# Reordering the recurrent stage of a one-core decoder kernel: paired 64-row products, swapped low-rank operands, norms on ScalarE

## What is computed

```python
xa = _ln(x, ln1_w, ln1_b)
sx = concat([state[:, 1:2] - xa[:, :1], xa[:, :-1] - xa[:, 1:]], axis=1)
xxx = tanh((xa + sx * maa_x) @ maa_w1).reshape(b, l, 5, DM)          # DM = 32
xm = xa + sx * (maa_stack + einsum('blfd,fde->blfe', xxx, maa_w2))   # 5 mixes: k, w, v, r, g
w = exp(-exp(time_decay + tanh(xw @ td_w1) @ td_w2))
r, k, v, g = xr @ Wr.T, xk @ Wk.T, xv @ Wv.T, silu(xg @ Wg.T)
s = a + w_t * s ; out = r_t . (u * a + s)                            # a = k_t v_t, a scan over time
x1 = x + groupnorm(out) * g @ Wo.T
xc = _ln(x1, ln2_w, ln2_b)                                           # then shifted and mixed with ffn_maa_k, ffn_maa_r
return x1 + sigmoid(xr2 @ Wfr.T) * (square(relu(xk2 @ Wfk.T)) @ Wfv.T)
```

## Time and profile before

| | |
|---|---|
| median of 3 runs | 3513.13 us (3513.01 to 3519.1) |
| profiled execution | 3515.94 us, of which the span from first to last instruction is 3514.2 us |
| TensorE matmul busy | 3222.5 us, 92% of the span |
| VectorE, ScalarE, GpSimd busy | 50%, 32%, 26% of the span |
| mean granted TensorE clock | 0.975 of full speed |
| the recurrent stage | from about 1571 to 2480 us of the span |

### The profile page before, as it was taken

The page is one execution under the profiler, slowest core; times in us unless marked ns, Lnnn a source line. Parts: engine busy times, 40 slices in busy tenths (PEclk is TensorE's granted clock), DMA queues, the critical chain, the costliest instruction groups (busy, mean ns, idle before and its releaser), DMA issues. The chain is left out here.

```text
span 3514.2 us, 52783 instructions
## 1 busy us (share of the span) xinstructions
PE 3222.5 (92%) x19344; PEld 2128.6 (61%) x19344; DVE 1748.5 (50%) x2503; ACT 1131.0 (32%) x4052; POOL 900.5 (26%) x614
## 2 busy tenths in 40 slices
PE   7999899989999888867899999997799999899999
PEld 5665556557666555546666666664455555466675
DVE  4555556510000378864788888888264454400000
ACT  2444234412111366642232332332133333311111
POOL 2333233300000022223555555565100000100000
PEclk9999999999999899988999999999899999999999
DMA  4110321110000141111011111110130110101010
GB/s 164 43 41 32 119 89 56 34 66 12 24 15 21 40 159 48 44 62 40 26 46 37 36 49 37 36 46 28 60 128 32 33 41 22 49 19 36 21 33 12
DMA packets 104308, 170.19 MB, mean 48 GB/s; under 512 B 16512, under 2 KB 54016, under 8 KB 100736
## 3 DMA queue, kind: packets, MB, share of 16 engines
q1 hardware_dynamic: 99296, 124.58, 11.1%
q10 hardware_dynamic: 4896, 44.04, 3.1%
HBM read 135.03 MB, written 33.55 MB: 48 GB/s over the span
## 5 line engine op out<-in xcount | busy, mean ns | idle before, releaser
L2396 POOL TENSOR_TENSOR rec_S<-rec_S,rec_r_t 128x1024 f32<-128x1024 f32 x128 | 309.8, 2421 | 315.1 <-DVE rec_S L2677 315.1
L2677 DVE TENSOR_TENSOR_SCAN rec_S<-rec_decay,rec_S 128x1024 f32<-128x1024 f32 x128 | 321.9, 2515 | 22.7 <-ACT rec_S L2466 19.4
L2076 PE MATMUL mlp_bank<-mlp_src_t,region_a 128*128 128x256 f32 x1024 | 224.8, 382 | 3.1 <-ACT mlp_src_t L1997 3.1
L2076 PE MATMUL pmlp_bank<-pmlp_src_t,region_a 128*128 128x256 f32 x1024 | 224.9, 382 | 1.9 <-ACT pmlp_src_t L1997 1.9
L2088 PE MATMUL mlp_bank<-region_a,mlp_h_t 128*128 128x512 f32 x512 | 221.1, 592 | 0.0
L2088 PE MATMUL pmlp_bank<-region_a,pmlp_h_t 128*128 128x512 f32 x512 | 221.1, 592 | 0.0
L2076 PEld LDWEIGHTS mlp_bank<-mlp_src_t,region_a 128*128 128x128 f32 x1024 | 196.5, 192 | 33.3 <-issue 6.8
L2076 PEld LDWEIGHTS pmlp_bank<-pmlp_src_t,region_a 128*128 128x128 f32 x1024 | 196.5, 192 | 32.0 <-issue 5.5
L1505 ACT ACTIVATE group_scores<-group_scores,group_negmax 128x128 f32<-128x128 f32 x512 | 197.6, 391 | 28.6 <-DVE group_negmax L1599 18.7
L2043 DVE TENSOR_TENSOR mlp_y<-mlp_bank,mlp_xres 128x512 f32<-128x512 f32 x16 | 11.1, 691 | 375.4 <-PE mlp_bank L2088 375.4
L2043 DVE TENSOR_TENSOR pmlp_y<-pmlp_bank,pmlp_xres 128x512 f32<-128x512 f32 x16 | 11.1, 691 | 364.6 <-PE pmlp_bank L2088 364.6
(11 more groups left out here) (363 smaller groups left out, 6496.4 us busy)
## 6 DMA issues: line engine op xcount, KB each, us to landing
rec_vb<-v_by_head SPq DMA_DIRECT2D x32, 512.0 KB, 4.2
region_a<-in_C_w ACTq DMA_DIRECT2D x2, 4096.0 KB, 20.5
region_a<-in_G_w ACTq DMA_DIRECT2D x2, 4096.0 KB, 19.5
self_xres<-in_x SPq DMA_DIRECT2D x16, 256.0 KB, 2.6
rows_A<-self_xres SPq DMA_DIRECT2D x16, 256.0 KB, 2.0
cross_ctx_t<-in_ctx_t SPq DMA_DIRECT2D x16, 256.0 KB, 3.3
cross_xres<-rows_A SPq DMA_DIRECT2D x16, 256.0 KB, 2.6
rows_B<-cross_xres SPq DMA_DIRECT2D x16, 256.0 KB, 2.0
```

Source lines behind the costliest of these rows:

```text
L2076: product = nc.tensor.matmul(ph.bank(item)[:, i * TT:(i + 1) * TT], W1[:, c, f:f + 128], src_t[:, c, :, :], start=c == 0, stop=c == C - 1)
L2396: nc.gpsimd.tensor_tensor(S[u % 4][:, :, :], S[u % 4][:, :, :], bcast(r_t[:, s.k, UNITS[u][0], :], [128, JH, T], 1), ALU.mult)\
L2677: nc.vector.tensor_tensor_scan(St[:, :, :].rearrange(flat), decay[m][:, :, :].rearrange(flat), St[:, :, :].rearrange(flat), 0.0, ALU.mult, ...
```

## The change

The low-rank product makes `xa_t` stationary and streams the 160 weight columns, so that its result has time on the partitions; one tanh writes it into `low_rows`, where each mix has 64 columns (32 values, a one, zeros); TensorE transposes these back in three products (`low_rank_t`, bank a, use lt) and ScalarE copies them into `low` (`low_rank_copy`). The mixes are placed so that 1 and 2, 3 and 4, and 0 and the decay product lie in different halves of the partitions; they are issued alternately in pairs. The two norms are applied by ScalarE as scale and bias; for that VectorE also negates the mean, and GpSimd multiplies it by the power. ScalarE copies `xa_t` back into bank b, from where `shift_front` takes one operand; that bank is now freed by the shift, and `low_rank` no longer waits for it. `gate` on ScalarE stands ahead of `bonus`, `make_gate` on VectorE ahead of `inputs(7)`. On TensorE the transposes of `ahead` stand before `ffn_keys`, the second half of r and of g directly behind the first, the first half of the output projection ahead of `sum_heads(2)`, and `ffn_gate` is split 2, 1, 1. The load of the first column (SyncE) waits for the same point of the former sequence, counted by three, now the copy back into the bank. Some lines of indentation are removed in the cut diff:

```diff
@@ -2167,12 +2167,12 @@
     MIX_AT = {f: at for at, f in enumerate(MIX_ORDER)}
-    MIX_TILE = {0: (0, 0), 1: (0, 64), 2: (1, 0), 3: (1, 64), 4: (2, 0)}
+    MIX_TILE = {1: (0, 0), 2: (0, 64), 0: (1, 0), 3: (1, 64), 4: (2, 0)}
...
     NEWTON = 10
-    SETUP = 11
+    SETUP = 7
@@ -2227,7 +2228,7 @@
         banks = StepBanks("rec", sem, {b: ps(f"bank_{b}", [128, BANK]) for b in "abcdn"}, [
-("a", "mx", 0), ("b", "mix1", 0), ("a", "mix2", 0), ("n", "mean", 2),
+("a", "mx", 0), ("a", "lt", 0), ("b", "mix1", 0), ("a", "mix2", 0), ("n", "mean", 2),
@@ -2373,9 +2373,12 @@
         def _(pool):
-def rsqrt(s, tile, out, var_done, out_done):
-    pool.wait_ge(var_done, s.n if tile is stats else s.n + 1)
+def rsqrt(n, tile, out, var_done, out_done):
+    pool.wait_ge(var_done, n + 1)
     nc.gpsimd.tensor_tensor(out[:, 0:1], tile[:, 9:10], minus_half[:, 0:1], ALU.pow).then_inc(out_done, 1)
+    pool.wait_ge(out_done, n * 2 + 1)
+    nc.gpsimd.tensor_tensor(out[:, 1:2], tile[:, 8:9], out[:, 0:1], ALU.mult).then_inc(out_done, 1)
@@ -2480,7 +2483,22 @@
                                     ACT.Identity, scale=vec("r_ln1_w", c), bias=vec("r_ln1_b", c))
-    last.then_inc(banks.free_sem("x"), 1)
+    last.then_inc(first_done, 1)
+    act.wait_ge(first_done, s.n * 3 + 2)
+    nc.scalar.activation(chunks(banks.bank("x")), xa_t[:, :, 1:T + 1], ACT.Copy).then_inc(first_done, 1)
+def normalise(n, out, rows, scale, scale_done, out_done):
+    act.wait_ge(scale_done, n * 2 + 2)
+    nc.scalar.activation(out[:, :], rows[:, :], ACT.Identity, scale=scale[:, 0:1], bias=scale[:, 1:2])\
+        .then_inc(out_done, 1)
+def normalise_front(s):
+    normalise(s.n - 1, x, x, rstd, rstd_done, xn_done)
+def normalise_back(s):
+    wait_count(act, stored, s.n * 16)
+    normalise(s.n, xn2, x1, rstd2, rstd2_done, xn2_done)
@@ -2495,12 +2513,16 @@
     full(act, s, "mx")
-    for at, f in enumerate(MIX_ORDER):
-        tile = MIX_TILE[f][0]
-        p0, col = ((0, 64, 32, 96)[f], 0) if f < 4 else (0, T)
-        last = nc.scalar.activation(low[tile][p0:p0 + DM, :], banks.bank("mx")[p0:p0 + DM, col:col + T],
-                                    ACT.Tanh)
-        last.then_inc(tanh_done if at < 4 else banks.free_sem("mx"), 1)
+    nc.scalar.activation(low_rows[:, :, 0:DM],
+                         banks.bank("mx")[:, 0:NMIX * DM].rearrange("p (f d) -> p f d", f=NMIX), ACT.Tanh)\
+        .then_inc(banks.free_sem("mx"), 1)
+def low_rank_copy(s):
+    full(act, s, "lt")
+    for tile in range(3):
+        p = 128 if tile < 2 else 64
+        last = nc.scalar.copy(low[tile][0:p, :], banks.bank("lt")[0:p, tile * T:(tile + 1) * T])
+        last.then_inc(low_done if tile < 2 else banks.free_sem("lt"), 1)
@@ -2568,6 +2590,7 @@
         low_rank_tanh(front)
+        low_rank_copy(front)
@@ -2588,6 +2611,8 @@
         first_states(middle, 5)
+    if back:
+        normalise_back(back)
@@ -2596,6 +2621,10 @@
         make_decay(front, 0)
+    if ahead and not is_first(ahead.n):
+        normalise_front(ahead)
+    if front:
+        gate(front)
@@ -2607,7 +2636,6 @@
     if front:
-        gate(front)
@@ -2623,30 +2651,22 @@
     dve.wait_ge(aggr_done, n + 1)
+    nc.vector.tensor_scalar(tile[:, 8:9], tile[:, 6:7], -1.0, None, ALU.mult)
     nc.vector.tensor_scalar(tile[:, 9:10], tile[:, 7:8], 1e-5, None, ALU.add).then_inc(var_done, 1)
-def norm_apply(n, out, rows, tile, scale, scale_done, out_done):
-    dve.wait_ge(scale_done, n + 1)
-    nc.vector.tensor_scalar(out[:, :], rows[:, :], tile[:, 6:7], scale[:, 0:1],
-                            ALU.subtract, ALU.mult).then_inc(out_done, 1)
...
-def normalise_front(s):
-    norm_apply(s.n - 1, x, x, stats, rstd, rstd_done, xn_done)
 def shift_front(s):
-    freed(dve, s, "x")
-    dve.wait_ge(first_done, s.n + 1)
-    nc.vector.tensor_tensor(sx_t[:, :, :], xa_t[:, :, 0:T], xa_t[:, :, 1:T + 1], ALU.subtract)\
-        .then_inc(sx_done, 1)
+    dve.wait_ge(first_done, s.n * 3 + 3)
+    nc.vector.tensor_tensor(sx_t[:, :, :], xa_t[:, :, 0:T], chunks(banks.bank("x")), ALU.subtract)\
+        .then_inc(banks.free_sem("x"), 1)
...
     if f == MIX_ORDER[0]:
-        dve.wait_ge(sx_done, s.n + 1)
+        freed(dve, s, "x")
@@ -2732,10 +2752,6 @@
     norm_stats(s.n, x1, stats2, touched2, back_norm)
-def normalise_back(s):
-    wait_count(dve, stored, s.n * 16)
-    norm_apply(s.n, xn2, x1, stats2, rstd2, rstd2_done, xn2_done)
@@ -2800,9 +2816,6 @@
         inputs(middle, 5)
-    if back:
-        normalise_back(back)
-    if middle:
@@ -2813,26 +2826,22 @@
         scan(middle, 6)
-    if ahead and not is_first(ahead.n):
-        normalise_front(ahead)
...
         mix_back(back, 1)
+    if front:
+        make_gate(front)
...
         shift_front(ahead)
-    if front:
-        make_gate(front)
...
     nc.vector.memset(tile[:, :, 0:1], 0.0)
-for tile in low:
-    last = nc.vector.memset(tile[:, :], 0.0)
-last.then_inc(zero_done, 1)
+nc.vector.memset(low_rows[:, :, :], 0.0).then_inc(zero_done, 1)
 dve.wait_ge(zero_done, 1)
-for tile, p in ((0, 32), (0, 96), (1, 0), (1, 64), (2, 32)):
-    nc.vector.memset(low[tile][p:p + 1, :], 1.0).then_inc(setup_done, 1)
+nc.vector.memset(low_rows[:, :, DM:DM + 1], 1.0).then_inc(setup_done, 1)
@@ -2894,43 +2903,44 @@
     begin(s, "mx")
-    freed(pe, s, "x")
-    pe.wait_ge(first_done, s.n + 1)
-    bank = banks.bank("mx")
+    pe.wait_ge(first_done, s.n * 3 + 2)
     parts = [(w, c, t) for w, t in ((maa_w1, 1), (w1_shift, 0)) for c in range(C)]
-    for lo, hi, at in ((0, 128, 0), (128, 160, T)):
-        for n, (w, c, t) in enumerate(parts):
-            last = nc.tensor.matmul(bank[0:hi - lo, at:at + T], w[:, c, lo:hi], xa_t[:, c, t:t + T],
-                                    start=n == 0, stop=n == len(parts) - 1)
+    for n, (w, c, t) in enumerate(parts):
+        last = nc.tensor.matmul(banks.bank("mx")[:, 0:NMIX * DM], xa_t[:, c, t:t + T], w[:, c, :],
+                                start=n == 0, stop=n == len(parts) - 1)
...
+def low_rank_t(s):
+    begin(s, "lt")
+    for tile in range(3):
+        p = 128 if tile < 2 else 64
+        last = nc.tensor.transpose(banks.bank("lt")[0:p, tile * T:(tile + 1) * T],
+                                   low_rows[:, 2 * tile:2 * tile + p // 64, :].rearrange("p f d -> p (f d)"),
+                                   ident)
+    done("lt", last)
+def mix_part(s, f, c):
+    tile, p0 = MIX_TILE[f]
+    last = nc.tensor.matmul(banks.bank(f"mix{f}")[:, c * 128:c * 128 + 128],
+                            mix_w[p0:p0 + 64, tile, c * 128:c * 128 + 128],
+                            low[tile][p0:p0 + 64, :], start=True, stop=True)
+    if c == C - 1:
+        done(f"mix{f}", last)
+def begin_mix(s, f):
+    begin(s, f"mix{f}")
+    if MIX_TILE[f][0] < 2:
+        pe.wait_ge(low_done, s.n * 2 + MIX_TILE[f][0] + 1)
+    else:
+        freed(pe, s, "lt")
...
-    for item in (f, g):
-        begin(s, f"mix{item}")
-    freed(pe, s, "mx")
+    begin_mix(s, f)
+    begin_mix(s, g)
     for c in range(C):
-        for item in (f, g):
-            tile, p0 = MIX_TILE[item]
-            last = nc.tensor.matmul(banks.bank(f"mix{item}")[:, c * 128:c * 128 + 128],
-                                    mix_w[p0:p0 + 64, tile, c * 128:c * 128 + 128],
-                                    low[tile][p0:p0 + 64, :], start=True, stop=True)
-            if c == C - 1:
-                done(f"mix{item}", last)
-def mix(s, f):
-    item = f"mix{f}"
-    begin(s, item)
-    if f == 4:
-        freed(pe, s, "mx")
-    else:
-        pe.wait_ge(tanh_done, s.n * 4 + MIX_AT[f] + 1)
-    tile, p0 = MIX_TILE[f]
-    for c in range(C):
-        last = nc.tensor.matmul(banks.bank(item)[:, c * 128:c * 128 + 128],
-                                mix_w[p0:p0 + 64, tile, c * 128:c * 128 + 128], low[tile][p0:p0 + 64, :],
-                                start=True, stop=True)
-    done(item, last)
+        mix_part(s, f, c)
+        mix_part(s, g, c)
@@ -2940,14 +2950,18 @@
-def decay_high(s):
+def decay_and_mix(s, f):
...
     freed(pe, s, "d")
+    begin_mix(s, f)
...
                                 start=True, stop=True)
-    done("z", last)
+        if c == C - 1:
+            done("z", last)
+        mix_part(s, f, c)
@@ -3042,71 +3056,69 @@
     if front:
+        low_rank_t(front)
+    if tail:
+        ffn_gate(tail, 2)
+    if front:
...
     if tail:
-        ffn_gate(tail, 1)
+        ffn_gate(tail, 3)
...
     if tail:
-        ffn_values(tail, 0)
+        ffn_values(tail, 0, 1)
...
     if tail:
-        ffn_values(tail, 1)
+        ffn_values(tail, 2, 3)
...
     if front:
-        decay_high(front)
+        decay_and_mix(front, 0)
...
     if front:
-        mix(front, 0)
...
         project(front, "v", 2, 1)
+    if back:
+        out_rows(back, 0, 1)
...
         sum_heads(middle, 2)
+    if front:
+        mix_pair(front, 3, 4)
     if back:
-        out_rows(back, 0)
-    if front:
-        mix(front, 3)
-    if back:
-        out_rows(back, 1)
```

(14 more changed lines are left out.)

42 lines of the change are left out of this document (21 added, 21 removed).

## The result

The changed kernel takes 3470.54 us in the median (3467.19 to 3475.03) beside 3514.97 for the kernel before on the same chip: ratio 0.9873, interval 0.9856 to 0.989, 44 us less. The forecast was 3483, the range 3455 to 3520. The profiled execution took 3469.47 (span 3467.6), 46.5 less than that of before.

The account below looks back on a forecast made before the run. The prediction took a step to be bound by a loop over TensorE, ScalarE, TensorE, VectorE, with GpSimd inside. Thirteen steps saving 1.9 us (24.7) plus 5 from filling, off 3513.1, gave 3483; range 3455 to 3520.

Parts of the forecast that it names:

- M: Point where VectorE starts `mix(front, 1)`, zero of a step; the next was forecast at 52.3 or 51.4 us.
- L: Point where TensorE starts `low_rank`; forecast at 46.5 or 45.6 us after M.
- Rival A: At the shared port `add_rows(4)` goes ahead of scan 5: step 50.5 us, total 3465; chance 17%.
- from L to M: Low-rank product to VectorE's first mix: falls from 6.87 to 5.8 us.
- B: Hand-overs throughout the step cost their upper bounds, so nothing comes of the change: 3507 to 3519 us; chance 15%.
- Rival C: TensorE's waits of 2.1 and 1.5 us make the granted clock fall each steady step: 3530 us, slower; chance 15%.
- two cases: Before the transposes, scan 6 gets between GpSimd's two front-norm operations (step 52.3 us) or does not (51.4).
- from M to `g`: `g` starts on TensorE 33.1 us after M, behind scan 4's end at 26.7 and a small GpSimd product of 0.38.
- the wait at the transposes: TensorE waits for bank b before the next rows' transposes: 1.5 us with scan 6 in between, otherwise 0.6.
- TensorE's own work: From `g` to L without waits: 11.9 us, staying as it is.
- the pair of 3 and 4: Mix 3 issued with mix 4 saves 1.08 us of TensorE, which then waits 2.1 for `g`.
- The filling: Three filling steps save about 1.3 us each from L to M, the set-up about 1: 5 us together.

Follow-up runs that it names:

- the two experiments above: Changed kernel with VectorE's bonus products moved ahead of scan 5: 3474.76 us; with bonus products and front statistics moved there: 3485.22 us.
- the two small parts undone that keep this wait: Changed kernel with mix 0 issued singly behind the decay's product: 3468.82 us; with the shift's operand from SBUF again: 3470.84 us.
- the three experiments with waits of 1.89 to 2.5: Changed kernel with bonus products ahead of scan 5: 3474.76 us; with front statistics there too: 3485.22; with both norms on VectorE: 3475.03.

## Why the prediction was right, and where not

**The mechanism came as forecast.** Counted from M of the step: `add_rows(4)` ends at 32.57 (33.0 forecast), `g` starts at 32.62 (33.1), scan 6 got between the two operations of GpSimd, the transposes start at 39.18 (40.0 in that case), L is at 45.73 (46.5), the next M at 51.19 (52.3). From `g` to L without the wait is 12.04 (11.9). Rival A needed `add_rows(4)` at 1.2 and is out by its row of 3.16. Where an experiment gave it that order (the back norm on VectorE), the step came to 50.52 (50.5 forecast for A), but that agreement is partly luck: counted from M (1969.69) L stood at 44.21 and not 44.75, and from L to M it was 6.31 and not 5.8, with a wait of 0.74 for GpSimd's product of unit 7 in it. B is out by the interval. The Trainium skill, "SBUF — State Buffer" (section "SBUF: two separate sides"), has the lock for which the first to start is served, and is silent on who goes when both wait. The rows agree with it if "start" is where a row begins, waiting included: the scan of 2005.61 goes ahead of `add_rows(4)` of 2006.76, and `add_rows` of 1993.41 ahead of the scan of 1993.43, which then takes 3.31. In these rows GpSimd's next operation begins only some 0.05 us before its former one ends, so a scan that has waited longer than that is first. The moved shift operand agrees as well: the product of unit 7 takes 2.37, and 2.73 with the operand back in SBUF.

**Rival C's event came once in fifteen steps.** Over the steady part the changed kernel shows one fall of the clock:

```profile
1700.00:1800.00 100.00, 91.43 (x694) 67.29 (x693) 86.00 (x120) 37.85 (x97) 65.56 (x42) 0.98 0.14 39
```

The clock goes to 0.50 just ahead of 1752.85, at the end of TensorE's wait of 1.98 before `g`, and is back before 1757; that step is 52.27 long, some 0.9 more than its neighbours. So C's event came in one step of fifteen, and its price was too high: 3.6 was read from one filling step, around which the clock was at half for some 17 us (from 1666 and from 1683), while the falls in the steady steps here and in the two experiments above cost 0.7 to 2.2. By the largest of them even a fall in each step would have left some of the 2.6 as a gain.

**The size of a step was off:** it fell by 2.6, not 1.9. I had taken the middle of two cases (52.3 and 51.4); the first came true, and its sum was 1.1 too long, in three terms:
- from M to `g`, 0.5: GpSimd's second operation puts 0.22 on the path (2004.22, where the power ends, to 2004.44) and not 0.38, and scan 4 ended at 26.52 and not 26.7. For the 26.7 the prediction gives no reason, and today's is 27.18 (2028.63 less 2001.45); the rows show that VectorE's waits of 0.44 for mix 3 (2021.40) and 0.25 for the mean (2004.12) in that stretch are gone.
- the wait at the transposes 1.07 and not 1.5. TensorE was ready at 38.1 (38.5 forecast), and the chain of ScalarE in front ended at 39.1 (40.0), although its norm is longer than I took it, 0.81 and not 0.63: GpSimd was done 0.7 sooner, for the reasons of the term above, and the three ScalarE operations overlap.
- from L to M 5.46 and not 5.8: three copies take 0.58 and not 0.85 (I had taken the 0.29 of a tanh for each), and `low_rank` with its tanh 2.37.

The terms for TensorE's own work were right (`g` to L 12.04 beside 11.9), the wait of 1.04 before `v` was (1.1), and the pair of 3 and 4 did what the sum says of it, nothing, since `add_rows(4)` sets `g`. Three small readings were off without weight in the sum: the exponentials before `v` end at 2013.22 and not at 2013.3, VectorE's wait for the first states of unit 7 did not grow by 1 to 2 us (1.42 beside 1.36), and B's costs of 1.7 leave 0.2 of the 1.9 and not 0.1.

**The number of steps was off too:** I counted thirteen; the gain runs through all fifteen. 36.4 / 15 = 2.43, less than 2.58, since the first four give less (1.6 to 2.4; the third, with 1.6, holds the fall of the clock). The last two gave 5.0 us, which I had left out as emptying.

**The filling gave 9.7 and not 5.** Its first chain from L to M fell from 9.48 (1578.71 to 1588.19) to 7.24 (1578.36 to 1585.60), 2.24 and not 1.3. I had priced the chain of the steady part, where the clock is at 1.00; in the filling it is not (0.59 over the same 8 us of the kernel before):

```profile
1580.65 1.97 PE L2909 MATMUL rec_bank_a<-rec_w_shift,rec_xa_t 128*128 128x160 f32 x8
```

```profile
1578.00:1586.00 8.00, 5.97 (x35) 5.30 (x35) 1.09 (x2) 1.80 (x6) 0.00 (x0) 0.74 0.24 93
```

The same eight passes take 1.25 in the steady step (at 2024.17) and 1.97 here, with a granted clock of 0.74 over these 8 us. With passes that long, halving their number is worth more. The set-up gave 0.35 (1578.71 to 1578.36), not 1. The rest of the 9.7 lies behind this chain: from the first M to the second L 3.2 less (30.44 to 27.27), where TensorE's wait of 3.74 for `make_gate` (1618.63) has gone and one of 1.83 for ScalarE's scaled rows (1612.87) stands, from the second L to its M 2.9 less (8.33 to 5.42), and 1.0 up to the `bonus_products`.

**What the prediction did not see** is which parts carried the gain. It has the gate in half a sentence ("the 1.17 us wait at L goes"); alone it is worth 27 us, as much as the low rank. And "nobody waits for the back norm" was true of its result and false of its place: on VectorE it was the filling that kept scan 5 out of the port until `add_rows(4)` had begun. I had the cost of taking it away (`add_rows(4)` 1.9 later) in the sum, but not the conclusion that leaving it would be better.

**What stays open:** in which step the granted clock falls. From 1700 to 2345 us of the fourteen traces it falls only in kernels in which TensorE waits some 1.9 us or more in one piece (the changed kernel, the two small parts undone that keep this wait, and the three experiments with waits of 1.89 to 2.5 before `g` or the transposes), and in none of the eight whose longest wait in the traced step is 1.38 or less. But most steps with the long wait show no fall: with the bonus products first TensorE's waits before `g` are the same (0.67 and 1.89) in a step that holds one and in the changed kernel's steps that hold none (0.69 and 1.89). No run here isolates what decides it.

## What to carry to other kernels

Before you take an operation off a busy engine, look at what it keeps apart: where two engines exclude each other, its duration sets who asks first, and a short operation in the right place is worth more than its time. Price each part against the wait that it ends in: a relieved engine that still idles (the norms), or saved passes in front of a longer wait (the pairs), are worth nothing, and a reordering without any saved work (the gate) can be worth as much as a new algorithm. When a meeting on a shared port is moved away from one unit, look at once for it at the next one. And read the granted clock of each step before you give a loss to an order.

## What the hardware showed that I had not expected

- A GpSimd operation issued while a scan waits is held until the scan ends: `add_rows` 3.16 instead of 1.18, the power on one column 2.54 instead of 0.54, the product on one column 2.17 instead of 0.19. Asked for 1.2, 0.7 and 0.4 us before GpSimd's operation ends, the scan won each time (2005.61, 2013.20, 2021.06), over an operation that stood next in GpSimd's order. Asked for 0.03 before the end, at 1993.43, 0.02 behind the start of `add_rows`, it lost and took 3.31 instead of 2.29.
- The granted clock fell to half inside a wait of TensorE of 1.89 us (about 1805, with the bonus products first), in a stretch in which TensorE is 91% busy. Such falls cost 0.7 to 2.2 us each here, and can outweigh what an order gains at the port: in the kernel with bonus products and statistics as filling they make up most of its loss.
- ScalarE's norm with a scale and a bias for each partition takes 0.81 to 0.84 us on 128 x 512, where its square or copy of the same shape takes 0.63 and 0.60.
